# Reordering the convolution stage of a four-layer network: third convolution one step later, three buffers for its input

## The chip, the core and the metric

The kernel runs on one core of a Trainium2 chip. Its engines are TensorE (PE in the profile, matmuls; PEld is its weight load), VectorE (DVE), ScalarE (ACT), GpSimd (POOL) and SyncE (SP). Each has its own instruction stream, and they meet through semaphores. SP and ACT also start transfers. The metric is the device time of one execution in microseconds; lower is better.

## What is computed

Sixty-four images of 16 channels, 128 x 128, pass through four layers. Each normalises its input over pairs of channels and adds its result to the input:

```
x = x + _L0_conv_ref(_gn(x), 5)      # Newton-Schulz inverse, 5 iterations, per channel
x = x + _L1_conv_ref(_gn(x), ...)    # 3x3 convolution of values quantised to whole numbers, scale, bias
x = x + _L2_conv_ref(_gn(x), ...)    # convolution along the diagonal, 5 taps
x = x + _L3_conv_ref(_gn(x), ...)    # 3x3 convolution that wraps around (done there by FFT)
```

The quantisation scale of layer 1 is a maximum over all images. So layer 0 of all images has to end before layer 1 of the first begins.

## The kernel before

The first stage (layer 0 for all images, lines up to 1060) takes about half of the time and is not touched. The second stage holds layers 1 to 3, and here the first, second and third convolution (numbers l = 1, 2, 3).

An image lies in SBUF as 128 partitions (8 rows by 16 channels) by 16 groups of rows by 128 columns. A convolution is worked out in four tiles (`BPI` = 4, index `u`) of 512 columns, each in one PSUM bank: `taps[l]` shifted band matrices on the normalised image `xn{l}`, then one product with the halo rows `xh{l}`, which transfers have gathered from `xn{l}`. Layer 1 needs one bf16 product for each shift, so 3 + 1 = 4 matmuls a tile. Layers 2 and 3 split values and weights into an upper and a lower fp16 part and need three products for each: 15 + 3 = 18 and 9 + 3 = 12 matmuls a tile. Six banks (`B_RING`) go round; `bank_free` makes PE wait for the evacuation of the tile that had the bank before.

What the other engines do for one image and one layer:

- DVE, `residual(l, n, u)` (lines 1251 to 1268): scales bank `u` and adds the layer's input. For l = 1 and 2 `chunk_stats` (1277) takes the statistics of the tile for the next layer, and `whole_stats` (1281) sums them.
- PE, `mean(l, n)` (1405): a small matmul of these sums with `gm`. DVE, `deviations` (1289 to 1299), five short instructions from it. PE, `var` (1410): a small matmul of their result, semaphore `spread`. DVE, `variance` (1303); ACT, `root` (1207); DVE, `normalise` (1312 to 1322), five short instructions and the scaling of the whole image into `F{l}`.
- ACT, `upper` (1202): the fp16 upper part. POOL, `lower` (1164): four instructions for the lower part. For l = 3 ACT copies borders, `wrap` (1192 to 1197), since this convolution wraps around. Then three halo transfers each go out on SP (1130) and on ACT (1184).
- Layer 1 has no statistics of its own here; `quantise` (1243 to 1248, DVE) makes `xn1` in three passes over the image, and ACT adds the bias in place (1214, in `first`) behind its three halo transfers.

The order on each engine is written out by hand, as a `step(s)` that every engine runs for s = 0 to 65 with layers of different images. In step s, PE does convolution 1 of image s, convolution 2 of s-1, convolution 3 of s-2. `mean` and `var` of layer 2 (image s) stand inside convolution 2, and those of layer 3 (image s-1) inside convolution 3. No engine may pass an instruction of its own that waits. The inputs of layers 2 and 3 lie in two buffers each (`x2_0`, `x2_1`, `x3_0`, `x3_1`); the output image takes the place of the third's input and is stored from there (1151), and `out_stored` makes the next writer wait for that store.

```
for u in range(BPI):
    conv(2, s, s - 1, h + odd - 1, 1 - odd, u,
         (lambda: mean(2, s)) if u == 1 and there(s) else None)
    if there(s) and u == 1:
        var(2, s)
```

Of the kernel before, what the change touches and what calls it, by code (L numbers as in the profile page):

```python
# [19 lines left out]
H = 128  # L20
C = 16
G = 8
CPG = C // G
RB = 8
NJ = H // RB
PW = H + 4
L = 2
# [14 lines left out]
def conv_net(nc, x, ident, gmat, gsel, w1, w1h, w2, w2h, w3, w3h, scale_w, bias, x1d, out):  # L42
# [39 lines left out]
    with keep:  # L82
# [982 lines left out]
        with ExitStack() as mem:  # L1065
# [4 lines left out]
            xs = [None, x1s] + [[sb(f"x{l}_{n}", [H, NJ, H]) for n in range(2)] for l in (2, 3)]  # L1070
# [15 lines left out]
            out_stored = [sem(f"out_stored{n}") for n in range(2)]  # L1086
# [16 lines left out]
            FIRST = 4  # L1103

            def run(eng, step):

                for s in range(FIRST):
                    step(s, s // 2, s % 2)
                images(step, FIRST, B - 2, 2)
                for s in range(B - 2, B + 2):  # L1110
                    step(s, s // 2, s % 2)

            def there(i):

                return not isinstance(i, int) or 0 <= i < B

            with nc.Block() as block:

                @block.sync
                def _(sp):  # L1120
                    def halos(l, n, odd):

                        if l == 3:
                            sp.wait_ge(wrapped, 2 * n + 2)
                        else:
                            sp.wait_ge(normed[l], n + 1)
                        for k, (row, shift, _) in enumerate(HALO[l][3:]):
                            r, at = row - RB, 2 * PW + L + shift
                            to = C * (k + 3)
                            sp.dma_start(xh[l][odd][to:to + C, :, 0:RUN],  # L1130
                                         xn[l][odd][C * r:C * r + C, :, at:at + RUN]).then_inc(halo[l][odd], 16)

                    def load(n, h, odd):
                        stand(sp, evac[1], BPI * (n - 1), w_loaded, 16 * 6)
                        sp.dma_start(xs[1][odd][:, :, :],
                                     x1d[n, :, :, 0:H].rearrange("j p w -> p j w")).then_inc(x1_in[odd], 16)

                    halos(1, 0, 0)

                    def step(s, h, odd):  # L1140
                        if there(s - 2):
                            halos(3, s - 2, odd)
                        if there(s + 2):
                            load(s + 2, h + 1, odd)
                        if there(s + 1):
                            halos(1, s + 1, 1 - odd)
                        if there(s):
                            halos(2, s, odd)
                        if there(s - 2):
                            stand(sp, evac[3], BPI * (s - 1), w_loaded, 16 * 6)  # L1150
                            sp.dma_start(out[s - 2, :, :, :], xs[3][odd][:, :, :]).then_inc(out_stored[odd], 16)

                    run(sp, step)
                    for n in range(2):
                        sp.wait_ge(out_stored[n], 16 * (B // 2))

                @block.gpsimd
                def _(pool):

                    def lower(l, n, odd):  # L1160

                        pool.wait_ge(high[l], n + 1)
                        for a in range(0, NJ, 4):
                            ins = nc.gpsimd.tensor_tensor(padded(xn[l][odd], 1)[:, a + 1:a + 5, L:L + H],  # L1164
                                                          F[l][:, a:a + 4, :],
                                                          padded(xn[l][odd], 0)[:, a + 1:a + 5, L:L + H],
                                                          ALU.subtract)
                        ins.then_inc(normed[l], 1)

                    def step(s, h, odd):  # L1170
                        if there(s):
                            lower(2, s, odd)
                        if there(s - 1):
                            lower(3, s - 1, 1 - odd)

                    run(pool, step)

                @block.scalar
                def _(act):
                    def halos(l, n, odd):  # L1180

                        for k, (row, shift, _) in enumerate(HALO[l][:3]):
                            r, at = row + RB, L + shift
                            act.dma_start(xh[l][odd][C * k:C * k + C, :, 0:RUN],  # L1184
                                          xn[l][odd][C * r:C * r + C, :, at:at + RUN]).then_inc(halo[l][odd], 16)

                    def wrap(i, odd):

                        v = xn[3][odd][:, :, :].rearrange("p s (j w) -> p s j w", w=PW)
# [9 lines left out]
                    def upper(l, n, odd):  # L1199

                        act.wait_ge(scaled_f[l], n + 1)
                        nc.scalar.activation(padded(xn[l][odd], 0)[:, 1:NJ + 1, L:L + H], F[l][:, :, :],  # L1202
                                             ACT.Copy).then_inc(high[l], 1)
# [6 lines left out]
                    def first(n, h, odd):  # L1210

                        act.wait_ge(normed[1], n + 1)
                        halos(1, n, odd)
                        nc.scalar.activation(xs[1][odd][:, :, :], xs[1][odd][:, :, :], ACT.Identity,
                                             bias=bst[:, 0:1]).then_inc(biased, 1)

                    def step(s, h, odd):
                        if there(s - 2):
                            wrap(s - 2, odd)
                            act.wait_ge(wrapped, 2 * s - 2)  # L1220
                            halos(3, s - 2, odd)
                        if there(s):
                            root(2, s)
                            upper(2, s, odd)
                        if there(s + 1):
                            first(s + 1, h + odd, 1 - odd)
                        if there(s):
                            act.wait_ge(normed[2], s + 1)
                            halos(2, s, odd)
                        if there(s - 1):  # L1230
                            root(3, s - 1)
                            upper(3, s - 1, 1 - odd)

                    first(0, 0, 0)
                    run(act, step)

                @block.vector
                def _(dve):
                    def quantise(n, h, odd):

                        dve.wait_ge(x1_in[odd], 16 * h + 16)
                        link = Link(dve, q_chain, 2 * n)
                        link.done(nc.vector.tensor_scalar(T[:, :, :], xs[1][odd][:, :, :], mcol[:, bass.ds(n, 1)],
                                                          acol[:, bass.ds(n, 1)], ALU.subtract, ALU.mult))
# [3 lines left out]
                        nc.vector.tensor_scalar(padded(xn[1][odd], 0)[:, 1:NJ + 1, L:L + H], T[:, :, :], MAGIC, -QMAX,  # L1248
                                                ALU.subtract, ALU.max).then_inc(normed[1], 1)

                    def residual(l, n, h, odd, u):

                        a, b = 4 * u, 4 * u + 4
                        bank = banks[(BPI * (l - 1) + u) % B_RING][:, :].rearrange("p (j w) -> p j w", w=H)
                        dst = xs[min(l + 1, 3)][odd][:, a:b, :]
                        dve.wait_ge(conv_ps[l], BPI * n + u + 1)
                        if l == 1:
                            if u == 0:
                                dve.wait_ge(biased, n + 1)
                            nc.vector.scalar_tensor_tensor(out=dst, in0=bank, scalar=sws[:, 0:1],  # L1260
                                                           in1=xs[1][odd][:, a:b, :], op0=ALU.mult,
                                                           op1=ALU.add).then_inc(evac[l], 1)
                        else:
                            if l == 2 and u == 0:
                                need(dve, out_stored[odd], 16 * h)
                            nc.vector.scalar_tensor_tensor(out=dst, in0=bank, scalar=wtop[l]["u"][:, 0:1],  # L1266
                                                           in1=xs[l][odd][:, a:b, :], op0=ALU.mult,
                                                           op1=ALU.add).then_inc(evac[l], 1)
# [5 lines left out]
                    def chunk_stats(l, n, odd, u):  # L1274

                        dve.wait_ge(evac[l - 1], BPI * n + u + 1)
                        nc.vector.bn_stats(bst_[l][:, u, :], xs[l][odd][:, 4 * u:4 * u + 4, :]).then_inc(gchain[l], 1)  # L1277
# [28 lines left out]
                    def normalise(l, n, odd):  # L1306

                        c = cols[l]
                        need(dve, normed[l], n)
# [12 lines left out]
                        nc.vector.tensor_scalar(F[l][:, :, :], xs[l][odd][:, :, :],  # L1322
                                                c["m"][:, 0:1], c["r"][:, 0:1], ALU.subtract,
                                                ALU.mult).then_inc(scaled_f[l], 1)
# [174 lines left out]
```

## Time and profile before

| What | Value |
|---|---|
| Median of three runs | 4287.48 us (4286.44 to 4287.55) |
| Span of the profiled execution, first to last instruction | 4285.7 us |
| Busy share of the span: PE, DVE, POOL, ACT | 98%, 80%, 56%, 48% |
| Second stage, from its first matmul | from 2277.1 us on |
| Mean granted TensorE clock of the core | 0.992 |

For the profiled execution no time of its own is given beside its span; the span is 1.8 us below the median of the runs. Busy time of PE is a poor measure by itself, since matmuls overlap. In the timeline what counts is the distance from one start to the next. A timeline row gives the start, the time from there to the end of the last instruction merged into it, engine, line, operation, result and inputs, shapes, and the number merged; in brackets stands the idle time before it, if it is worth telling, and what ended it.

### The profile page before, as it was taken

How to read it: one execution, taken by the hardware profiler on the slowest of the kernel's cores; microseconds unless marked ns; L12 is line 12 of the kernel's file. 1: busy time of each engine (PE TensorE's matmuls, PEld its weight loads, DVE VectorE, ACT ScalarE, POOL GpSimd, SP SyncE). 2: the span in 40 equal slices, each digit the busy share in tenths (PEclk: the TensorE clock that was granted, in tenths of full speed). 3: DMA queues.
4: the chain of work that ended last, by engine and by line, in shares of the span. 5: the costliest groups of instructions: out<-in, count | busy, mean ns of one | idle time of the engine just before them, and what ended most of it. 6: DMA issues, size and time to landing. Idle time of an engine off the chain costs nothing. (4 is left out here: it accounts for less than half of the span.)

```text
span 4285.7 us, 81705 instructions
## 1 busy us (share of the span) xinstructions
PE 4194.6 (98%) x30409; PEld 3108.7 (73%) x30409; DVE 3444.2 (80%) x7393; ACT 2072.5 (48%) x4296; POOL 2407.9 (56%) x3149
## 2 busy tenths in 40 slices
PE   7999999999999999999996999999999999999998
PEld 7999999999999999999992444444444444444443
DVE  6888888888888888888876787878787888888784
ACT  5776777777777777777761222222222222222221
POOL 6888888888888888888871222222222222222221
PEclk9999999999999999999997999999999999999999
DMA  2221222222222222222214555555555555555553
GB/s 69 64 62 55 65 65 60 60 60 60 60 66 65 60 63 68 60 60 60 60 41 97 133 137 134 137 133 137 134 138 134 138 134 138 134 138 134 138 134 84
DMA packets 333657, 404.28 MB, mean 94 GB/s; under 512 B 23088, under 2 KB 286032, under 8 KB 316880
## 3 DMA queue, kind: packets, MB, share of 16 engines
q1 hardware_dynamic: 308688, 334.25, 30.8%
q10 hardware_dynamic: 24576, 64.79, 5.6%
q8 instruction: 246, 4.03, 0.4%
q14 instruction: 147, 1.20, 0.1%
HBM read 135.22 MB, written 134.22 MB: 63 GB/s over the span
## 5 line engine op out<-in xcount | busy, mean ns | idle before, releaser
L1392 PE MATMUL bank<-xn,wt 128*128 128x512 f16 (+1 forms) x6912 | 1661.6, 381 | 19.9 <-issue 10.7
L1164 POOL TENSOR_TENSOR xn<-F,xn 128x512 f16<-128x512 f32 x512 | 541.6, 1090 | 1453.2 <-ACT xn L1202 1453.2
L1392 PEld LDWEIGHTS bank<-xn,wt 128*128 128x128 f16 (+1 forms) x6912 | 672.9, 100 | 805.0 <-issue 21.9
L463 ACT ACTIVATE P<-bank 128x512 f32<-128x512 f32 x1024 | 606.8, 608 | 264.0 <-PE bank L962 154.5
L1266 DVE SCALAR_TENSOR_TENSOR x<-bank,wu,x 128x512 f32<-128x512 f32 x512 | 382.4, 747 | 313.7 <-PE bank L1399 306.6
L1202 ACT ACTIVATE xn<-F 128x2048 f16<-128x2048 f32 x128 | 244.9, 1913 | 603.3 <-DVE F L1322 603.3
L1399 PE MATMUL bank<-xh,wth 96*128 96x512 f16 (+1 forms) x1792 | 515.6, 380 | 12.1 <-DMA xh<-xn 12.1
L313 POOL TENSOR_TENSOR W<-W 128x512 f16<-128x512 f32 x256 | 290.3, 1166 | 145.7 <-ACT W L489 145.7
L1277 DVE BATCH_NORM_STATS2 bs<-x 128x6 f32<-128x512 f32 x512 | 355.6, 695 | 17.7
L569 DVE BATCH_NORM_STATS2 st<-X 128x6 f32<-128x256 f32 x1024 | 351.5, 411 | 5.8 <-DMA X<-in_x 5.7
L1399 PEld LDWEIGHTS bank<-xh,wth 96*128 96x128 f16 (+1 forms) x1792 | 174.2, 97 | 232.6 <-DMA xh<-xn 15.7
L358 POOL TENSOR_TENSOR S<-P 128x512 f32<-128x512 f32 x256 | 317.8, 1272 | 32.0 <-ACT P L463 31.6
L369 POOL TENSOR_TENSOR P<-P,idt 128x512 f32<-128x512 f32 x256 | 318.4, 1278 | 29.0 <-ACT P L463 28.8
L353 POOL TENSOR_TENSOR YX<-idt,YX 128x512 f32<-128x512 f32 x256 | 324.1, 1278 | 5.5 <-ACT YX L453 5.5
L498 ACT ACTIVATE W<-X,nb,r 128x256 f32<-128x256 f32 x512 | 259.4, 590 | 134.2 <-POOL nb L341 130.7
L1207 ACT ACTIVATE sd<-ve 128x1 f32<-128x1 f32 x128 | 26.1, 204 | 608.9 <-DVE ve L1303 603.0
L364 POOL TENSOR_TENSOR S<-S,P 128x512 f32<-128x512 f32 x256 | 318.1, 1274 | 0.0
L453 ACT ACTIVATE YX<-bank,cs 128x128 f32<-128x128 f32 x1024 | 277.7, 381 | 11.8 <-PE bank L894 3.5
L673 DVE SCALAR_TENSOR_TENSOR X<-bank,cout,X 128x128 f32<-128x128 f32 x1024 | 270.5, 344 | 12.9 <-PE bank L988 12.9
L607 DVE TENSOR_TENSOR P<-bank,idt 128x512 f32<-128x512 f32 x256 | 177.0, 692 | 109.0 <-PE bank L979 103.2
L929 PE MATMUL bank<-YX 128*128 128x128 f32 x2048 | 260.9, 276 | 0.0
L944 PE MATMUL bank<-P 128*128 128x128 f32 x2048 | 260.2, 277 | 0.0
(129 smaller groups left out, 7619.3 us busy)
## 6 DMA issues: line engine op xcount, KB each, us to landing
X<-in_x SPq DMA_DIRECT2D x64, 1024.0 KB, 4.8
x_scratch<-X SPq DMA_DIRECT2D x64, 1024.0 KB, 5.6
X<-x_scratch SPq DMA_DIRECT2D x64, 1024.0 KB, 8.8
out<-x SPq DMA_DIRECT2D x64, 1024.0 KB, 3.9
xh<-xn SPq DMA_DIRECT2D x384, 131.8 KB, 4.5
xh<-xn ACTq DMA_DIRECT2D x384, 131.8 KB, 5.4
xh<-xn SPq DMA_DIRECT2D x192, 65.9 KB, 3.2
xh<-xn ACTq DMA_DIRECT2D x192, 65.9 KB, 2.7
```

The lines of the kernel that those rows point to most:

```text
L313: nc.gpsimd.tensor_tensor(W16[:, 1, at, :], W[:, at, :], W16[:, 0, at, :], ALU.subtract).then_inc(w_lower, 1)
L353: nc.gpsimd.tensor_tensor(e, eyes, e, ALU.subtract).then_inc(a_new, 1)
L358: nc.gpsimd.tensor_tensor(quad(S, q), quad(P1, q), quad(P2, q), ALU.add).then_inc(s_new, 1)
L364: nc.gpsimd.tensor_tensor(quad(S, q), quad(S, q), quad(P3, q), ALU.add).then_inc(q_new, 1)
L369: nc.gpsimd.tensor_tensor(quad(P2, q), quad(P2, q), eyes, ALU.add).then_inc(r_new, 1)
L463: nc.scalar.activation(into[:, 4 * q:4 * q + 4, :], banks[q][:, :].rearrange("p (m w) -> p m w", m=4), ACT.Copy).then_inc(sb, 1)
L569: ins = nc.vector.bn_stats((st0, st1)[k][:, g, :], group_of(X[slot], g))
L1164: ins = nc.gpsimd.tensor_tensor(padded(xn[l][odd], 1)[:, a + 1:a + 5, L:L + H], F[l][:, a:a + 4, :], padded(xn[l][odd], 0)[:, a + 1:a + 5, ...
L1266: nc.vector.scalar_tensor_tensor(out=dst, in0=bank, scalar=wtop[l]["u"][:, 0:1], in1=xs[l][odd][:, a:b, :], op0=ALU.mult, op1=ALU.add).the ...
L1277: nc.vector.bn_stats(bst_[l][:, u, :], xs[l][odd][:, 4 * u:4 * u + 4, :]).then_inc(gchain[l], 1)
L1392: nc.tensor.matmul(bank, wt[l][:, a, k, :], v, start=(k == a == b == 0), stop=False)
L1399: ins = nc.tensor.matmul(bank, wth[l][:, a, :], v, start=False, stop=(a, b) == products[-1])
```

## The change

The steps are laid out anew. PE now does convolution 1 of image s, then convolution 3 of s-3 (it was s-2), then convolution 2 of s-1; there are 67 steps and not 66. The two small matmuls of layer 2 (image s) stand in convolution 3, after its tiles 1 and 3. Those of layer 3 (image s-2) stand ahead of convolution 3 and after its tile 0. DVE's order follows: convolution 1's residuals with `deviations(3, s-2)` among them, then `variance(3)`, `quantise(s+1)`, `normalise(3, s-2)`, then convolution 3's residuals with `deviations(2, s)`, `variance(2)`, `normalise(2, s)` among them, then convolution 2's. ACT adds the bias and sends the halo of image s+1 before `root(2, s)`. Three buffers hold layer 3's input. Bank and predecessor of each tile come from a list of the whole order. Matmuls, element operations, transfers and the engine of each are the same, and so is the first stage.

```diff
-            xs = [None, x1s] + [[sb(f"x{l}_{n}", [H, NJ, H]) for n in range(2)] for l in (2, 3)]
+            THIRD = 3
+            xs = [None, x1s] + [[sb(f"x{l}_{n}", [H, NJ, H]) for n in range(k)] for l, k in ((2, 2), (3, THIRD))]
...
+            LATE = (None, 0, 1, 3)
+            STEPS = B + LATE[3]
...
+            order = [(l, s - LATE[l], u) for s in range(STEPS) for l in (1, 3, 2) if there(s - LATE[l]) for u in range(BPI)]
+            place = {piece: k for k, piece in enumerate(order)}
...
                 def _(sp):
...
+                    for s in range(STEPS):
+                        if there(s - 1):
+                            sp.wait_ge(normed[2], s)
+                            halo_copies(sp, 2, s - 1, False)
+                        if there(s + 2):
+                            load(s + 2)
+                        if there(s + 1):
+                            sp.wait_ge(normed[1], s + 2)
+                            halo_copies(sp, 1, s + 1, False)
+                        if there(s - 3):
+                            store(s - 3)
                         if there(s - 2):
...
+                            sp.wait_ge(wrapped, 2 * (s - 1))
+                            halo_copies(sp, 3, s - 2, False)
...
                 def _(act):
...
+                    first(0)
+                    for s in range(STEPS):
+                        if there(s - 1):
+                            act.wait_ge(normed[2], s)
+                            halo_copies(act, 2, s - 1, True)
                         if there(s - 2):
...
+                            root(3, s - 2)
+                            upper(3, s - 2)
+                        if there(s + 1):
+                            first(s + 1)
                         if there(s):
                             root(2, s)
-                            upper(2, s, odd)
...
+                            upper(2, s)
+                        if there(s - 2):
+                            wrap(s - 2)
+                            act.wait_ge(wrapped, 2 * (s - 1))
+                            halo_copies(act, 3, s - 2, True)
...
                 def _(dve):
...
+                    quantise(0)
+                    for s in range(STEPS):
+                        for u in range(BPI):
+                            if u == BPI - 1 and there(s - 2):
+                                deviations(3, s - 2)
+                            if there(s):
+                                residual(1, s, u)
+                                chunk_stats(2, s, u)
                         if there(s):
...
                             whole_stats(2, s)
+                        if there(s - 2):
+                            variance(3, s - 2)
+                        if there(s + 1):
+                            quantise(s + 1)
+                        if there(s - 2):
+                            normalise(3, s - 2)
                         for u in range(BPI):
...
+                            if there(s - 3):
+                                residual(3, s - 3, u)
                             if there(s):
                                 if u == 0:
                                     deviations(2, s)
-                                if u == 1:
+                                if u == 2:
                                     variance(2, s)
...
+                                if u == 3:
+                                    normalise(2, s)
+                        for u in range(BPI):
+                            if there(s - 1):
+                                residual(2, s - 1, u)
+                                chunk_stats(3, s - 1, u)
                         if there(s - 1):
                             whole_stats(3, s - 1)
...
                 def _(pe):
...
+                    for s in range(STEPS):
                         if there(s):
                             for u in range(BPI):
...
+                                conv(1, s, u)
+                        if there(s - 2):
+                            mean(3, s - 2)
+                        for u in range(BPI):
+                            if there(s - 3):
+                                conv(3, s - 3, u)
+                            if there(s - 2) and u == 0:
+                                var(3, s - 2)
+                            if there(s):
+                                if u == 1:
+                                    mean(2, s)
+                                if u == 3:
+                                    var(2, s)
                         if there(s - 1):
                             for u in range(BPI):
...
+                                conv(2, s - 1, u)
```

The program of the changed kernel shows what this makes of two engines. First PE, in one of the last full steps before the change: convolution 1's last tile, then the beginning of convolution 2 (bank 6 takes the small matmuls of layer 2, bank 7 those of layer 3).

```order
L1399 MATMUL bank3<-xh1_1,wth1 128x512
L1392 MATMUL bank4<-xn2_0,wt2 128x512 x15
L1399 MATMUL bank4<-xh2_0,wth2 128x512 x3
L1392 MATMUL bank5<-xn2_0,wt2 128x512 x6
L1405 MATMUL bank6<-s2,gm 128x1
L1392 MATMUL bank5<-xn2_0,wt2 128x512 x9
L1399 MATMUL bank5<-xh2_0,wth2 128x512 x3
L1410 MATMUL bank6<-q2,gm 128x1
L1392 MATMUL bank0<-xn2_0,wt2 128x512 x15
```

The same engine after the change, from the small matmul behind convolution 1 to the first matmuls of convolution 2 (L1371 and L1376 are the convolution's lines now, L1382 is `mean`, L1387 `var`):

```order
L1382 MATMUL bank7<-s3,gm 128x1
L1371 MATMUL bank0<-xn3_0,wt3 128x512 x9
L1376 MATMUL bank0<-xh3_0,wth3 128x512 x3
L1387 MATMUL bank7<-q3,gm 128x1
L1371 MATMUL bank1<-xn3_0,wt3 128x512 x9
L1376 MATMUL bank1<-xh3_0,wth3 128x512 x3
L1382 MATMUL bank6<-s2,gm 128x1
L1371 MATMUL bank2<-xn3_0,wt3 128x512 x9
L1376 MATMUL bank2<-xh3_0,wth3 128x512 x3
L1371 MATMUL bank3<-xn3_0,wt3 128x512 x9
L1376 MATMUL bank3<-xh3_0,wth3 128x512 x3
L1387 MATMUL bank6<-q2,gm 128x1
```

The small matmul of `q2`, which waits for DVE's `deviations(2)`, has moved from the inside of convolution 2 to the place right ahead of it, and all of convolution 2 stands behind it.

DVE before the change, around `deviations(2)`, which ends with `q2`:

```order
L1277 BN_STATS bs2<-x2_0 128x6
L1281 TENSOR_REDUCE s2<-bs2 128x1
L1266 SCALAR_TENSOR_TENSOR x3_1<-bank4,wu2,x2_1 128x512
L1277 BN_STATS bs3<-x3_1 128x6
L1289 TENSOR_TENSOR dv2<-bs2,bank6 128x8
L1291 COPY m2<-bank6 128x1
L1293 TENSOR_TENSOR dv2<-dv2 128x8
L1295 SCALAR_TENSOR_TENSOR dv2<-bs2,dv2 128x8
L1299 TENSOR_REDUCE q2<-dv2 128x1
```

DVE after it (L1256 is every residual, L1270 `whole_stats`, L1237 to L1242 `quantise`, L1300 to L1311 `normalise`, L1278 to L1288 `deviations`):

```order
L1270 TENSOR_REDUCE s2<-bs2 128x1
L1292 TENSOR_SCALAR ve3<-bank7 128x1
L1237 TENSOR_SCALAR T<-X1,mcol,acol 128x2048
L1240 TENSOR_SCALAR T<-T 128x2048
L1242 TENSOR_SCALAR xn1_1<-T 128x16x128
L1300 RECIPROCAL ra3<-sd3 128x1
L1302 TENSOR_TENSOR rb3<-ra3 128x1
L1304 TENSOR_TENSOR rb3<-rb3,ve3 128x1
L1306 TENSOR_SCALAR rb3<-rb3 128x1
L1308 TENSOR_TENSOR r3<-ra3,rb3 128x1
L1311 TENSOR_SCALAR F3<-x3_0,m3,r3 128x2048
L1256 SCALAR_TENSOR_TENSOR x3_2<-bank0,wu3,x3_2 128x512
```

`deviations(2)` follows behind the last of these rows. Between `s2` and it there stood one residual with its statistics; now there stand `variance(3)`, the three passes of `quantise`, `normalise(3)` and one residual.

## Rows read from the trace of the kernel before

**Rows 1.** Windows: busy us and instructions of each engine, clock, DMA, one step.

```profile
3217.34:3247.87 30.53, 30.48 (x145) 13.99 (x144) 24.59 (x49) 7.48 (x9) 8.46 (x8) 1.00 0.57 136
```

**Rows 2.** Timeline of PE, convolution 2, 3 and 1 of a step.

```profile
3226.30 0.38 PE L1405 MATMUL bank<-s,gm 128*128 128x1 f32 x2
3226.54 2.12 PE L1392 MATMUL bank<-xn,wt 128*128 128x512 f16 x9
...
3233.20 3.43 PE L1392 MATMUL bank<-xn,wt 128*128 128x512 f16 x15
...
3237.12 2.13 PE L1392 MATMUL bank<-xn,wt 128*128 128x512 f16 x9
...
3247.87 0.82 PE L1392 MATMUL bank<-xn,wt 128*128 128x512 bf16 x3
...
3251.39 3.43 PE L1392 MATMUL bank<-xn,wt 128*128 128x512 f16 x15
```

**Rows 3.** Timeline of DVE in the same stretch.

```profile
3220.43 0.75 DVE L1260 SCALAR_TENSOR_TENSOR x<-bank,sws,X 128x512 f32<-128x512 f32 x1
...
3221.82 0.73 DVE L1260 SCALAR_TENSOR_TENSOR x<-bank,sws,X 128x512 f32<-128x512 f32 x1
...
3226.16 0.75 DVE L1266 SCALAR_TENSOR_TENSOR x<-bank,wu,x 128x512 f32<-128x512 f32 x1
...
3227.56 0.14 DVE L1289 TENSOR_TENSOR dv<-bs,bank 128x8 f32<-128x8 f32 x1
...
3228.21 0.16 DVE L1299 TENSOR_REDUCE q<-dv 128x1 f32<-128x8 f32 x1
...
3230.74 0.14 DVE L1303 TENSOR_SCALAR ve<-bank 128x1 f32<-128x1 f32 x1
...
3234.58 0.16 DVE L1312 RECIPROCAL ra<-sd 128x1 f32<-128x1 f32 x1
...
3235.54 1.35 DVE L1322 TENSOR_SCALAR F<-x,m,r 128x2048 f32<-128x2048 f32 x1
3236.81 0.75 DVE L1266 SCALAR_TENSOR_TENSOR x<-bank,wu,x 128x512 f32<-128x512 f32 x1
...
3248.07 0.75 DVE L1266 SCALAR_TENSOR_TENSOR x<-bank,wu,x 128x512 f32<-128x512 f32 x1 [1.94 <-PE bank L1399]
3248.74 0.15 DVE L1312 RECIPROCAL ra<-sd 128x1 f32<-128x1 f32 x1
```

**Rows 4.** Timeline of POOL and DVE, where both are busy.

```profile
3238.91 4.23 POOL L1164 TENSOR_TENSOR xn<-F,xn 128x512 f16<-128x512 f32 x4 [12.14 <-ACT xn L1202]
...
3241.63 0.49 DVE L1293 TENSOR_TENSOR dv<-dv 128x8 f32<-128x8 f32 x1
3242.16 1.01 DVE L1295 SCALAR_TENSOR_TENSOR dv<-bs,dv 128x8 f32<-128x8 f32 x1
```

**Rows 5.** Timeline, start of the stage, to PE's first step with all three convolutions.

```profile
2281.36 0.61 PE L1399 MATMUL bank<-xh,wth 96*128 96x512 bf16 x1 [2.80 <-DMA xh<-xn]
...
2288.17 0.16 DVE L1281 TENSOR_REDUCE s<-bs 128x1 f32<-128x8 f32 x1
...
2300.38 0.61 PE L1399 MATMUL bank<-xh,wth 96*128 96x512 bf16 x1 [4.40 <-DMA xh<-xn]
...
2305.69 3.43 PE L1392 MATMUL bank<-xn,wt 128*128 128x512 f16 x15
...
2362.64 0.82 PE L1392 MATMUL bank<-xn,wt 128*128 128x512 bf16 x3
```

**Rows 6.** Timeline, end of the program, from the last of the full steps on.

```profile
4224.67 3.43 PE L1392 MATMUL bank<-xn,wt 128*128 128x512 f16 x15
...
4253.05 1.34 DVE L1322 TENSOR_SCALAR F<-x,m,r 128x2048 f32<-128x2048 f32 x1
...
4268.99 1.46 PE L1399 MATMUL bank<-xh,wth 96*128 96x512 f16 x3 [3.54 <-DMA xh<-xn]
4270.24 4.05 PE L1392 MATMUL bank<-xn,wt 128*128 128x512 f16 x9
```

More of the change, by code:

```diff
@@ L1102, in conv_net, with xs_of, bank_of, halo_copies @@
             CH = 9
[L1103 to L1111, printed above, removed]
-            def there(i):
-                return not isinstance(i, int) or 0 <= i < B
+            LATE = (None, 0, 1, 3)
+            STEPS = B + LATE[3]
+            def there(i):
+                return 0 <= i < B
+            def xs_of(l, n):
+                return xs[l][n % len(xs[l])]
+            order = [(l, s - LATE[l], u) for s in range(STEPS) for l in (1, 3, 2) if there(s - LATE[l]) for u in range(BPI)]
+            place = {piece: k for k, piece in enumerate(order)}
+            def bank_of(l, n, u):
+                return banks[place[l, n, u] % B_RING]
+            def halo_copies(eng, l, n, above):
+                for k, (row, shift, _) in enumerate(HALO[l]):
+                    if (row < 0) == above:
+                        r, at = row % RB, (0 if row < 0 else 2 * PW) + L + shift
+                        eng.dma_start(xh[l][n % 2][C * k:C * k + C, :, 0:RUN],
+                                      xn[l][n % 2][C * r:C * r + C, :, at:at + RUN]).then_inc(halo[l][n % 2], 16)
             with nc.Block() as block:
@@ L1120, in _ @@
                 def _(sp):
[L1121 to L1131, printed above, removed]
@@ L1153, in _, with load, store @@
-                    run(sp, step)
-                    for n in range(2):
-                        sp.wait_ge(out_stored[n], 16 * (B // 2))
+                    def load(n):
+                        stand(sp, evac[1], BPI * (n - 1), w_loaded, 16 * 6)
+                        sp.dma_start(xs_of(1, n)[:, :, :],
+                                     x1d[n, :, :, 0:H].rearrange("j p w -> p j w")).then_inc(x1_in[n % 2], 16)
+                    def store(n):
+                        sp.wait_ge(evac[3], BPI * (n + 1))
+                        sp.dma_start(out[n, :, :, :], xs_of(3, n)[:, :, :]).then_inc(out_stored[n % THIRD], 16)
@@ L1171, in step @@
                         if there(s):
[L1172 to L1176, printed above, removed]
+                            lower(2, s)
                 @block.scalar
                 def _(act):
[L1180 to L1185, printed above, removed]
@@ L1256, in residual @@
                         dve.wait_ge(conv_ps[l], BPI * n + u + 1)
[L1257 to L1268, printed above, removed]
+                        if l == 1 and u == 0:
+                            dve.wait_ge(biased, n + 1)
@@ L1348, in step @@
+                        for u in range(BPI):
+                            if there(s - 1):
+                                residual(2, s - 1, u)
+                                chunk_stats(3, s - 1, u)
                         if there(s - 1):
                             whole_stats(3, s - 1)
-                        for u in range(BPI):
-                            if there(s - 2):
-                                residual(3, s - 2, hb, before, u)
-                            if there(s - 1):
-                                if u == 0:
-                                    deviations(3, s - 1)
-                                if u == 2:
-                                    variance(3, s - 1)
-                                if u == 3:
-                                    normalise(3, s - 1, prev)
@@ L1377, in conv, with bank_free @@
-                    def conv(l, s, n, h, odd, u, between=None):
-                        bank = banks[(BPI * (l - 1) + u) % B_RING][:, :]
+                    def bank_free(l, n, u):
+                        k = place[l, n, u] - B_RING
+                        if k >= 0:
+                            m, i, v = order[k]
+                            pe.wait_ge(evac[m], BPI * i + v + 1)
+                    def conv(l, n, u):
+                        bank = bank_of(l, n, u)[:, :]
                         if u == 0:
```

149 lines of the change are left out of this document (42 added, 107 removed).

## The prediction, as it was made before the run

> **What bounds the kernel now.** I read the windows first. One step of the second stage lasts 30.53 us, PE is busy for 30.48 us of it at full clock, and DVE for 24.59 us [rows 1]. So PE bounds the steady part, and a new order of the same work can win next to nothing there. The timeline of PE then tells what a step holds. A tile of convolution 2 takes 3.92 us (3233.20 to 3237.12). Convolution 3 with two small matmuls in it takes 10.75 us (3237.12 to 3247.87), and convolution 1 takes 3.52 us (3247.87 to 3251.39) [rows 2]. Four tiles of convolution 2 are 15.67 us. 15.67 + 10.75 + 3.52 = 29.94 us; the other 0.59 us are the two small matmuls in convolution 2, the first of which waits a little for DVE and costs 0.24 us once it starts (3226.30 to 3226.54) [rows 2]. Full steps follow each other from 2362.64 us [rows 5] to 4224.67 us [rows 6]: 1862.0 us for 61 steps, 30.53 each. Any wait of PE that the new order puts into a step counts 61 times; the rest is the start and the drain.
>
> **The steady step, laid out by hand.** The place to look at is the small matmul of `q2`. It now stands ahead of all of convolution 2, and DVE has much to do before it delivers `q2`. Let 0 be the moment at which PE ends the last tile of convolution 2 and begins convolution 1. DVE has been idle there (it needs about 1.4 us a tile against 3.92) and starts 0.20 us later: 3248.07 against 3247.87 [rows 2, 3]. From there DVE never waits, so its instructions follow at the distances in rows 3:
> - last tile of convolution 2 and `whole_stats(3)`: a residual with statistics takes 1.38 us (3220.43 to 3221.82), and four of these with the sum 5.73 us (3220.43 to 3226.16), so the sum adds 0.20. DVE is at 0.20 + 1.38 + 0.20 = 1.78.
> - three tiles of convolution 1: 3 x 1.38 = 4.15, to 5.93. PE has ended these tiles by 2.6 us, so none is waited for.
> - `deviations(3)`: 0.65 to its last instruction (3227.56 to 3228.21), 0.16 for that, and the next starts 0.08 behind its start: to 6.66; `q3` is there at 6.74.
> - fourth tile and `whole_stats(2)`: 1.58, to 8.24.
> - `variance(3)` and `quantise`: 3.84 (3230.74 to 3234.58), to 12.08.
> - `normalise(3)`: 2.23 (3234.58 to 3236.81), to 14.31. Its root on ACT has 3.8 us beside `quantise`.
> - one residual without statistics: 0.67 (3248.07 to 3248.74), to 14.98.
> - `deviations(2)`: 0.65 + 0.16, so `q2` is there at 15.79.
>
> PE has 3.52 us of convolution 1, the small matmul of `s3` (about 0.15), and 10.75 us of convolution 3. On its way it meets `q3`: tile 0 of convolution 3 ends at about 3.67 + 2.62 = 6.29, and `q3` comes at 6.74, so it loses 0.5 and the slower start of a matmul that waited, 0.1. It stands at the matmul of `q2` at about 15.0. `q2` comes 0.8 us later. With 0.06 for the semaphore and the 0.24 of a waiting small matmul, convolution 2 starts at 16.1, and the step ends at 16.1 + 15.67 = 31.8 us. I take 31.78. The first wait (for `q3`) is swallowed by the second, since DVE and not PE sets the time of `q2`. What bounds a step is then a ring: last tile of convolution 2, DVE's row of work, `q2`, convolution 2. The step is 1.25 us longer, 61 x 1.25 = 76 us.
>
> **What is moved and costs nothing.** Layer 3 gets a whole step between `normalise(3)` and its convolution. From the start of `F` to the landed halo this chain took 15.94 us at the end of the program (4253.05 to 4268.99) [rows 6]; in the new step it starts at 13.0 and would end at 29, but its border copies stand behind `upper(2)` on ACT, which puts them some 4 us later: 33. PE asks for this halo at 31.8 + 5.6 = 37.4, in tile 0 of the next step. This is the thinnest cover, 4 us; a halo later than that adds what it is late. ACT's queue is the other: the bias of image s+1 and its three transfers now stand ahead of `root(2)`. DVE's `normalise(2)` waits there from about 17.8 to about 20, and behind it are the residuals of convolution 2. It has to end before 31.98 less three tiles, 27.8, so 5 us of slack cover it; past that each us costs one. The image for `quantise` is loaded a step ahead, the store has a step more through the third buffer, and all banks come free 1.5 us or more before PE asks. On SP each transfer stands behind a wait that is over by then. These I cost at nothing.
>
> **Start and drain.** Before, the first full step starts at 2362.64 [rows 5]. In the new order DVE ends the sum for image 0 at 2288.17 as before, quantises image 1 at once (to 2292), and then comes ACT's work (three transfers and the bias, about 4.2 us) ahead of the root; `normalise(2, 0)` ends at about 2298.8. PE can finish convolution 1 of image 1 at about 2292.0 + 4.3 (wait of 2.80 for the halo and three cold matmuls [rows 5]) + 5.3 (2300.38 to 2305.69) = 2301.6. Four tiles on DVE, `quantise` and `deviations` end at 2298.8 + 5.7 + 3.8 + 0.8 = 2309.1; `q2` blocks convolution 2 here too. It starts at 2309.5 and not at 2305.69, and ends at 2325.2 or, with a clock fallen to half after such idle time, 2.4 us later. Step 2 has no convolution 3, and lasts 31.1 us with PE idle for most of the first 15; again up to 2.4 us for the clock. (Cold matmuls take 1.25 us for three, 4268.99 to 4270.24 [rows 6], against 0.65 warm; some 12 of them are 2.4 us.) So the first full step starts between 2356 and 2361; I take 2361, since PE idles in both places. The 61 full steps end at 2361 + 61 x 31.78 = 4299.6. Step 64 has no convolution 1: about 2.2 us until `s3`, 10.6, 15.67, together 28.5. Then `F` of the last image starts 6.5 us after its convolution 2 (tile and sum 1.8, small matmul, `deviations`, root and five short instructions), its halo lands 15.9 later, and from there on it is as before: 4285.7 - 4269.0 = 16.7. Together 39.1. The end is 4299.6 + 28.5 + 39.1 = 4367.2, against the profiled span of 4285.7: 81.5 more. The median of the runs is 1.8 above that span, so 4287.5 + 81.5 = 4369; with the last tiles a little warmer than before I say **4368 us**.
>
> **Rivals.** (1) *DVE and POOL meet.* In the old order `deviations` meets POOL's `lower` once a step, and two of its instructions take 0.49 and 1.01 us [rows 4] where both take about 0.2 without POOL [rows 3]; the second ends within 0.1 us of POOL's end (3238.91 + 4.23). If this happened to `deviations(2)` in the new order, it would add some 1.15 us to the ring: 4368 + 61 x 1.15 = 4438. It speaks against it that POOL starts 3.37 us after the start of `F` (3235.54 to 3238.91 [rows 3, 4]), so at 13.04 + 3.37 = 16.4 in my step, 0.6 us after `q2`. The rival decides if DVE is over 0.6 us later between `F` and `q2` than I have it. The Trainium skill (SBUF — State Buffer, Who interferes with whom) says that a DVE instruction with two SBUF inputs and a GpSimd one that reads SBUF share a read path which one holds for its whole instruction; the trace agrees, with 1.01 us for an instruction that takes 0.17 alone.
>
> (2) *Not slower.* *PE stays the bound.* If DVE delivered `q2` 0.8 us earlier than I have it, and `q3` 0.5 us earlier, PE would stay the bound: 29.94 us, which hold two of the small matmuls, and two more at about 0.14 make 30.22 us a step, less than the 30.53 now, because the wait in front of the matmul at 3226.30 [rows 2] goes too. Then 2361 + 61 x 30.22 + 28.5 + 39.1 = 4272, or **4274** as a median, 0.3% faster than before. The point from which this decides is a DVE row of 15.0 us from the end of convolution 2 to `q2`. For it: it needs only 5% less. Against it: every distance in the row was measured in the same chain of instructions without idle time.
>
> (3) *The clock falls* in the new pauses of under 1 us. If only one tile of convolution 2, 18 matmuls, ran at half clock, each step would lose 3.7 us: 4594. A wait of this kind is in the old order with 0.2 us only and the clock stayed at 1.00 [rows 1].
>
> **How the numbers follow.** The forecast has 83%, the meeting with POOL 6%, the PE-bound step 9%, the clock 2%. The forecast's own bounds are 0.4 us a step either way (24 us: some distances are read from other pairs of instructions) and 6 us for the start and drain: about 4340 to 4400. This holds its 83% nearly whole; the others lie outside, and the range ends there. About 0.2% (8.6 us) is what a measurement of this kernel can tell from no change. Slower: the forecast, POOL and the clock, 91%. The PE-bound step is faster by over 0.2% where both waits vanish (5%), and within 0.2% where 0.1 to 0.3 us of them stay in each step (4%).
>
> **What would show it.** Right: a window of one step of 31.8 us with PE idle before L1387 for 0.4 to 0.5 us and again for 0.8, released by DVE's L1288; DVE without idle time from the last residual of convolution 2 to L1288, idle before `normalise(2)` for about 2 us, released by ACT. POOL's first instruction starts after L1288 has ended. Wrong: a PE that waits on halo transfers, on `normed`, or on banks; L1284 at 1 us; a clock below 1.00 in the steady part; or a step of 30.2 to 30.5 us.

## The result, and the profile after

The changed kernel takes 4371.28 us (4371.05 to 4372.48, 4 runs) against 4286.96 us before (4286.03 to 4287.55, 4 runs). The ratio is 1.0198, with a 95% interval of 1.0184 to 1.0213: slower by 84 us. The profiled execution spans 4369.8 us.

The windows view of one full step after the change answers to [rows 1] (columns as there: window, length, busy us and instructions of PE, PEld, DVE, ACT and POOL, clock, DMA share, GB/s).

```profile
3218.88:3250.64 31.76, 30.73 (x145) 13.91 (x144) 25.00 (x49) 7.24 (x9) 8.47 (x8) 1.00 0.56 131
```

The same 145 matmuls at the same clock of 1.00 now take 31.76 us and not 30.53. The waits view of the changed kernel, from 2400 to 4250 us, names what PE waits for (in total, times, longest):

```profile
DVE x L1256 <- PE bank L1376: 300.6, 175, 2.4
PEld bank L1387 <- DVE q L1288: 117.1, 116, 1.2
PE bank L1387 <- DVE q L1288: 60.2, 117, 0.7
DVE ra L1300 <- ACT sd L1203: 36.7, 58, 0.7
```

PEld's row is the weight load of the same matmul, which overlaps PE. There are two waits a step (117 in 58 steps), both of the small matmul of `q` (L1387) for the last of DVE's `deviations` (L1288). The timeline of PE shows where they are (in brackets: idle time before, and what ended it). It answers to [rows 2]:

```profile
3218.88 0.82 PE L1371 MATMUL bank<-xn,wt 128*128 128x512 bf16 x3
...
3224.50 0.81 PE L1376 MATMUL bank<-xh,wth 96*128 96x512 f16 x3
3225.69 0.38 PE L1387 MATMUL bank<-q,gm 128*128 128x1 f32 x2 [0.38 <-DVE q L1288]
3225.93 2.13 PE L1371 MATMUL bank<-xn,wt 128*128 128x512 f16 x9
...
3233.28 0.81 PE L1376 MATMUL bank<-xh,wth 96*128 96x512 f16 x3
3234.74 0.38 PE L1387 MATMUL bank<-q,gm 128*128 128x1 f32 x2 [0.65 <-DVE q L1288]
3234.98 3.43 PE L1371 MATMUL bank<-xn,wt 128*128 128x512 f16 x15
...
3250.64 0.82 PE L1371 MATMUL bank<-xn,wt 128*128 128x512 bf16 x3
```

Three halo matmuls take 0.65 us from start to next start, so convolution 3 ends at 3233.93 and the small matmul starts 0.81 us later (the bracket says 0.65, since the modelled end of a matmul lies after its successor's start). DVE's timeline in the same step answers to [rows 3], and POOL's first row stands with it:

```profile
3219.08 0.75 DVE L1256 SCALAR_TENSOR_TENSOR x<-bank,wu,x 128x512 f32<-128x512 f32 x1 [2.44 <-PE bank L1376]
...
3225.47 0.16 DVE L1288 TENSOR_REDUCE q<-dv 128x1 f32<-128x8 f32 x1
...
3230.98 0.16 DVE L1300 RECIPROCAL ra<-sd 128x1 f32<-128x1 f32 x1
...
3231.94 1.35 DVE L1311 TENSOR_SCALAR F<-x,m,r 128x2048 f32<-128x2048 f32 x1
...
3234.32 0.17 DVE L1284 SCALAR_TENSOR_TENSOR dv<-bs,dv 128x8 f32<-128x8 f32 x1
3234.52 0.16 DVE L1288 TENSOR_REDUCE q<-dv 128x1 f32<-128x8 f32 x1
...
3237.35 0.16 DVE L1300 RECIPROCAL ra<-sd 128x1 f32<-128x1 f32 x1 [0.63 <-ACT sd L1203]
3237.55 0.96 DVE L1302 TENSOR_TENSOR rb<-ra 128x1 f32<-128x1 f32 x1
3238.55 1.01 DVE L1304 TENSOR_TENSOR rb<-rb,ve 128x1 f32<-128x1 f32 x1
```

```profile
3235.31 4.23 POOL L1169 TENSOR_TENSOR xn<-F,xn 128x512 f16<-128x512 f32 x4 [19.51 <-ACT xn L1198]
```

From 3219.08, where convolution 2 has released it, DVE has no idle time until it delivers `q2`. It first waits behind that, before `normalise(2)` (0.63 us, for the root on ACT). `deviations` runs at its short durations, since POOL begins 0.63 us after L1288 has ended. It is `normalise(2)` that meets POOL: L1302 and L1304 take 0.96 and 1.01 us where 0.16 is usual (L1300, ahead of them, still takes it). PE does not wait for that: its next tiles follow each other without a gap, and DVE is idle again before the second residual of convolution 2, from 3242.71 to 3243.01.

### The profile page after: what moved, and what is told of

It is laid out like the page before. It is cut to its first block and busy times, and to the rows that moved or that the text cites. A ratio compares the mean times of both kernels' runs of the same rounds, so it can differ in the third digit from the quotient of the medians.

```text
span 4369.8 us, 81640 instructions
## 1 busy us (share of the span) xinstructions
PE 4217.2 (97%) x30409; PEld 3105.2 (71%) x30409; DVE 3470.4 (79%) x7393; ACT 2055.8 (47%) x4296; POOL 2407.3 (55%) x3149
## 5 line engine op out<-in xcount | busy, mean ns | idle before, releaser
L1371 PE MATMUL bank<-xn,wt 128*128 128x512 f16 (+1 forms) x6912 | 1649.4, 383 | 7.7 <-DVE xn L1242 5.2
L1371 PEld LDWEIGHTS bank<-xn,wt 128*128 128x128 f16 (+1 forms) x6912 | 674.5, 100 | 797.9 <-issue 21.6
L1256 DVE SCALAR_TENSOR_TENSOR x<-bank,wu,x 128x512 f32<-128x512 f32 x512 | 375.6, 746 | 368.5 <-PE bank L1376 368.3
L1376 PE MATMUL bank<-xh,wth 96*128 96x512 f16 (+1 forms) x1792 | 515.8, 380 | 8.3 <-DMA xh<-xn 8.3
L1376 PEld LDWEIGHTS bank<-xh,wth 96*128 96x128 f16 (+1 forms) x1792 | 174.5, 97 | 228.8 <-DMA xh<-xn 10.6
```

Source lines behind the costliest of these rows:

```text
L1256: nc.vector.scalar_tensor_tensor(out=dst, in0=bank, scalar=col[:, 0:1], in1=xs_of(l, n)[:, at, :], op0=ALU.mult, op1=ALU.add).then_inc(eva ...
L1371: nc.tensor.matmul(bank, wt[l][:, a, k, :], v, start=(k == a == b == 0), stop=False)
L1376: ins = nc.tensor.matmul(bank, wth[l][:, a, :], v, start=False, stop=(a, b) == products[-1])
```

## Experiments

Two theories stood against each other. Mine: DVE's row of work between the end of convolution 2 and `q2` closes a ring with convolution 2, and the place of the small matmuls decides. The rival: the order as such (the steps, the third buffer, the transfers) costs the time, and the wait is only where it shows. All kernels but one start from the changed kernel.

**q2's small matmul behind tile 0 of convolution 2.**

```diff
-                                if u == 3:
-                                    var(2, s)
-                        if there(s - 1):
-                            for u in range(BPI):
+                        for u in range(BPI):
+                            if there(s - 1):
                                 conv(2, s - 1, u)
+                            if there(s) and u == 0:
+                                var(2, s)
```

> The changed order, with the small matmul of q2 moved on PE from ahead of convolution 2 to behind its tile 0. My theory (the ring through DVE's row and q2 sets the step): the wait of 0.8 us and the slower small matmul behind it go, the wait for q3 (0.54 + 0.10 us) stays, so the step falls from 31.76 to about 30.85 us; with some 10 us less at the start, where q2 no longer blocks convolution 2, about 4306 us. Rival (the longer step comes from the order as such, the third buffer or the transfers, and the wait is only where it shows): the wait reappears elsewhere and the time stays near 4371.

Measured: 4306.62 us (4305.68 to 4310.10, 3 runs). The order, the buffers and the transfers are those of the changed kernel, so the rival falls. The step is 30.85 us (from 2354.63 to 2385.48, the starts of convolution 1), as expected, with the one wait for `q3` in it. That the median comes out at the expected 4306 is in part chance: in the profiled execution, the longest of the three (4310.10), the start is 6.6 us shorter than in the changed kernel and not 10.

**The opposite way round: DVE's `deviations(2)` ahead of `normalise(3)`, PE untouched.**

```diff
                             quantise(s + 1)
+                        if there(s):
+                            deviations(2, s)
                         if there(s - 2):
                             normalise(3, s - 2)
...
-                                if u == 0:
-                                    deviations(2, s)
```

> The changed order, with DVE's deviations(2) moved ahead of normalise(3) and the residual; PE as in the changed kernel. My theory: q2 is there at about 12.9 us of the step, before PE asks at 15.0, so only the wait for q3 stays; 30.85 us a step, about 4314 us. Rival (order as such): near 4371.

Measured: 4314.40 us (4313.24 to 4315.55, 2 runs), step 30.84 us (2358.10 to 2388.94). The wait can be taken away from either end. The profiled execution spans 4311.6 us and that of the run before 4308.4. These 3.2 us lie ahead of the first full step (2358.10 against 2354.63). The medians are 8 us apart, but the three executions of the run before differ by 4.4 us among themselves, and no trace shows where the rest beyond the 3.2 us lies.

**Only q3's small matmul moved.**

```diff
-                            if there(s - 2) and u == 0:
+                            if there(s - 2) and u == 1:
                                 var(3, s - 2)
```

> The changed order, with only the small matmul of q3 moved, behind tile 1 of convolution 3; q2 stays ahead of convolution 2. My theory (DVE's row sets q2): PE waits less for q3, but DVE's variance(3) gets its value 0.96 us later, at 9.2 us of the step, and all behind it down to q2 moves by that; step 32.7 us, about 4429 us, slower although a wait is gone. Rival (each wait of PE costs its own length): 0.64 us less a step, about 4332 us.

Measured: 4513.56 us (4513.31 to 4513.82, 2 runs). A wait of PE is gone, and the kernel is 142 us slower. This settles that waits don't simply add up here, but the size was off by 85 us. The timeline of PE in this kernel shows both parts:

```profile
3216.76 0.82 PE L1371 MATMUL bank<-xn,wt 128*128 128x512 bf16 x3
...
3230.61 0.81 PE L1376 MATMUL bank<-xh,wth 96*128 96x512 f16 x3
3233.58 0.38 PE L1387 MATMUL bank<-q,gm 128*128 128x1 f32 x2 [2.17 <-DVE q L1288]
3233.83 5.09 PE L1371 MATMUL bank<-xn,wt 128*128 128x512 f16 x15
3238.76 0.81 PE L1376 MATMUL bank<-xh,wth 96*128 96x512 f16 x3
3239.41 3.43 PE L1371 MATMUL bank<-xn,wt 128*128 128x512 f16 x15
...
3251.15 0.82 PE L1371 MATMUL bank<-xn,wt 128*128 128x512 bf16 x3
```

`q2`'s matmul starts at 3233.58 - 3216.76 = 16.82 us of the step, where the ring puts it (15.86 + 0.96). But after 2.3 us without matmuls tile 0 of convolution 2 takes 5.58 us (3233.83 to 3239.41) and the next one its usual 3.92. The first matmuls run at 1.2 GHz and not at 2.4: the windows view has a granted clock of 0.65 for the 15 matmuls of this tile (3233.83 to 3238.76), and of 0.95 over 400 us of the kernel:

```profile
3200.00:3600.00 400.00, 376.17 (x1689) 169.05 (x1688) 291.88 (x569) 84.41 (x106) 101.31 (x96) 0.95 0.51 121
```

Sixty of the 61 full steps hold this pause (in the last there is no `quantise` of a next image ahead of `deviations(2)`, and `q2` is there in time). In 8 of the 60 the matmuls behind it are not slow, and the step lasts 32.73 us, just what was expected. The other 52 last 34.36 us in the mean: 52 x 1.63 = 85 us, which is the missing amount. Why the same pause costs in one step and not in another is not shown.

**Both small matmuls of q moved** (the first and the third edit together).

> As the run before, and the small matmul of q3 behind tile 1 of convolution 3 instead of tile 0. My theory: no wait of PE is left in a step, 30.2 us, about 4267 us, less than the kernel before the change (4287). Rival (order as such): not below 4350.

Measured: 4278.61 us (4275.20 to 4279.96, 9 runs), ratio to the kernel before the change 0.9977 (0.9966 to 0.9987). So the new order beats the old one once no small matmul stands before its input. It beats it by less than I said. The full steps run from 2357.06 to 4207.48 us, 30.33 us each and not 30.2: `q3`'s and `s2`'s small matmuls now stand in a row, and take 0.37 us from the start of the first to the next tile, where two apart take 0.14 each:

```profile
3214.53 0.28 PE L1387 MATMUL bank<-q,gm 128*128 128x1 f32 x2
3214.68 0.36 PE L1382 MATMUL bank<-s,gm 128*128 128x1 f32 x2
3214.90 2.13 PE L1371 MATMUL bank<-xn,wt 128*128 128x512 f16 x9
```

The 0.09 us more are 5.5 us in 61 steps. Some 2 us come from four single steps that are 0.3 to 0.9 us longer; in three of them PE waits 0.3 to 0.8 us for the halo in tile 0 of convolution 3 (at 3302.91, 3727.95 and 4152.50). The start (from the stage's first matmul to the first full step, 2278.53 to 2357.06) is 6.5 us shorter than in the changed kernel (2276.17 to 2361.18), where I had expected 10 for the move of `q2`'s matmul.

**Meeting POOL.** Rival 1 of the prediction asked what happens if `deviations(2)` comes later on DVE. Two kernels put it behind one and behind two more residuals:

```diff
-                                if u == 0:
+                                if u == 1:
                                     deviations(2, s)
```

> The changed order, with DVE's deviations(2) behind one more residual of convolution 3. My theory of the ring without POOL: q2 comes 0.66 us later, and so does the step, 32.4 us, about 4411 us. DVE's L1284 would end at 16.3 us of the step and POOL's lower begins at 16.4. If the two engines meet already here: over 33 us a step, about 4470 us.

Measured: 4408.45 us (4407.93 to 4408.97, 2 runs), step 32.43 us (2392.72 to 2425.15). The ring follows DVE by exactly the one residual, and PE's pause of 1.5 us leaves the clock at 1.00. POOL starts at 3219.84, 0.16 us after the end of L1284, so the two just miss each other.

```diff
-                                if u == 0:
+                                if u == 2:
                                     deviations(2, s)
-                                if u == 2:
+                                if u == 3:
                                     variance(2, s)
-                                if u == 3:
                                     normalise(2, s)
```

> The changed order, with DVE's deviations(2) behind two more residuals, so that its two-input instructions fall into POOL's lower. If an instruction of DVE with two inputs in SBUF waits there for the running one of POOL's four: q2 at about 18.8 us of the step, 34.7 us a step, about 4551 us. If the two do not disturb each other: 1.33 us more than the changed kernel, 33.1 us, about 4452 us.

Measured: 4718.30 us (4717.63 to 4718.97, 2 runs). The timelines of DVE and POOL in this kernel (POOL's row holds three of its four instructions, to the end of the stretch shown):

```profile
3243.88 3.18 POOL L1169 TENSOR_TENSOR xn<-F,xn 128x512 f16<-128x512 f32 x3 [25.10 <-ACT xn L1198]
3244.00 0.98 DVE L1282 TENSOR_TENSOR dv<-dv 128x8 f32<-128x8 f32 x1
3245.02 1.01 DVE L1284 SCALAR_TENSOR_TENSOR dv<-bs,dv 128x8 f32<-128x8 f32 x1
3246.07 0.16 DVE L1288 TENSOR_REDUCE q<-dv 128x1 f32<-128x8 f32 x1
```

DVE's L1282 starts 0.12 us after POOL's first instruction and ends 1.10 us after that start, when POOL's first (1.06 us) is over, and L1284 ends with POOL's second; the reduction, which reads one tensor, is not held. The Trainium skill (SBUF — State Buffer, Who interferes with whom) calls the read and write ports that DVE shares with GpSimd an exclusive lock, and says that a DVE instruction with two SBUF inputs contends with a GpSimd one that reads SBUF. The trace agrees: 0.98 and 1.01 us for two instructions that take 0.17 each without POOL. `q2`'s matmul starts at 18.84 us of the step (3246.28 - 3227.44), where 18.8 was expected. The 167 us that the kernel is slower than expected are the clock again, as PE's timeline shows:

```profile
3246.28 0.58 PE L1386 MATMUL bank<-q,gm 128*128 128x1 f32 x2 [3.62 <-DVE q L1288]
3246.73 6.02 PE L1370 MATMUL bank<-xn,wt 128*128 128x512 f16 x15
3252.59 0.81 PE L1375 MATMUL bank<-xh,wth 96*128 96x512 f16 x3
3253.24 3.43 PE L1370 MATMUL bank<-xn,wt 128*128 128x512 f16 x15
```

Tile 0 takes 6.51 us and not 3.92. The 2.6 us more are 158 us in 61 steps, and 4551 + 158 = 4709. The small matmul itself is slow too (0.45 us to the next start and not 0.24), which adds 13 us at most; with it the sum is 4722, 4 us over the measured time.

**What the old order leaves.** The wait of 0.2 us before the matmul at 3226.30 [rows 2] is in the kernel before. One edit there moves the small matmul of `s2` three matmuls on:

```diff
-                            if between and k == 1:
+                            if between and k == (2 if l == 2 else 1):
                                 between()
```

> The kernel before the change, with one edit: the small matmul of s2 stands after nine matmuls of tile 1 of convolution 2 instead of six. Theory: the old step holds one wait of 0.22 us and 0.10 us of slower start, which go: 30.2 us a step, 61 x 0.32 = 19.5 us, about 4267.5 us. Rival (the wait only moves to q2 or to DVE's chain): 4287.

Measured: 4266.04 us (4265.89 to 4271.84, 4 runs), ratio 0.9953 (0.9938 to 0.9967). The full step is 30.21 us (2366.30 to 4209.15, 61 steps), 0.32 less than before.

**All small matmuls of the new order off their waits.** `s3` and `q3` behind tiles 0 and 1 of convolution 3, `q2` as in the first experiment:

```diff
-                        if there(s - 2):
-                            mean(3, s - 2)
                         for u in range(BPI):
                             if there(s - 3):
                                 conv(3, s - 3, u)
-                            if there(s - 2) and u == 0:
-                                var(3, s - 2)
+                            if there(s - 2):
+                                if u == 0:
+                                    mean(3, s - 2)
+                                if u == 1:
+                                    var(3, s - 2)
```

> The changed order, with q2's small matmul behind tile 0 of convolution 2, and those of s3 and q3 behind tiles 0 and 1 of convolution 3. Theory: step 30.2 us as with q2 and q3 moved alone, and at the end PE no longer stands before s3 in the steps without convolution 1, where it idled twice for 1.8 us and then ran some 3.5 us at half clock: 7 us less than that run, about 4260 us. Rival (the idle time at the end is only moved, since the last image's chain sets the end): about 4267 us.

Measured: 4271.46 us (4269.74 to 4272.64, 5 runs), 7.1 us less than with the two of `q` alone. I had expected 4260, which was 7 us less than the 4267 expected of that run, and that run had missed its 4267. Part of the gain is where it was expected: from the end of the full steps to the end of the span it is 65.6 us (4203.75 to 4269.3) and not 70.6 (4207.48 to 4278.1). These are 5.0 of the 8.8 us between the two profiled spans. The other 3.7 lie ahead of the end of the full steps (2.9 of them ahead of the first, 2354.18 against 2357.06) and were not expected. So the near match of 7.1 with the 7 expected is in part chance.

Last, `s2`'s matmul behind tile 2, so that no two stand in a row:

```diff
-                                if u == 1:
+                                if u == 2:
                                     mean(2, s)
```

> As the run with all three small matmuls moved, and that of s2 behind tile 2 of convolution 3 instead of tile 1, where it stood right behind q3's. Theory: two small matmuls in a row cost 0.36 us against 0.28 apart, and with them apart the full step falls from 30.32 us to 30.21, 61 x 0.11 = 6.7 us; about 4265 us, level with the old order with its one edit (4266) or a little less. Rival (the step is held by DVE's row by now): 4271.

Measured: 4266.17 us (4264.13 to 4268.11, 4 runs), ratio 0.9952 (0.9935 to 0.9968); step 30.22 us (2355.16 to 4198.75, 61 steps). The best new order and the old one with its one edit can't be told apart: with these places of the small matmuls, the order of the convolutions is worth nothing that can be measured.

## Why the prediction was right

The forecast was 4368 us, and 4371.28 was measured. Point by point:

- **The ring.** `q2` was put at 15.79 us of the step, and L1288 ends at 3234.52 + 0.16 - 3218.88 = 15.80. `q3` was put at 6.74, and comes at 6.75. Convolution 2 was to start at 16.1, and does at 3234.98, which is 16.10. The step was to be 31.78 and is 31.76. The full steps carry 75 us of the 84. The other 9 are the two ends: the first full step begins 1.5 us earlier than before (2361.18 against 2362.64), and from the end of the full steps to the end of the span it is 71.4 us and not 61.0.
- **The first wait is swallowed by the second.** Right, by the kernel with only `q3`'s matmul moved: with this wait gone, `q2` came no sooner but 0.96 us later.
- **The POOL rival.** POOL was put at 16.4 us, and starts at 16.43. As forecast, it did not happen. But the rival's own numbers were off. It was to decide at 0.6 us, counted to the end of `q2`; the run with one more residual was 0.67 us later and missed POOL. Both runs fit if it is the last instruction with two inputs in SBUF that counts, L1284, which ends at 3234.49, 0.82 us ahead of POOL. The price was put at 1.15 us a step, and the meeting costs 1.65 in the run with two more residuals (0.98 and 1.01 us against 0.17 each), because both instructions fall wholly into POOL's. Its total of 4438 was too low for that reason, and more so because the clock falls too.
- **ACT's queue.** `normalise(2)` was to wait about 2 us for the root, and waited 0.63; ACT's three transfers and bias take less than I had added up, since the three are issued (3233.33 to 3235.18) while ACT works on `upper(3)` (3233.32 to 3235.23). That the two engines would meet there was not foreseen. There was slack for all of it.
- **Third layer's halo.** No wait of PE for a halo is in the full steps, as said. That this is the thinnest cover shows in the shorter steps of the experiments, where PE waited for it a few times.
- **The PE-bound rival.** Its condition did not come about, but its step of 30.22 us was right: it is the step of the last experiment, in which no small matmul waits.
- **The clock rival.** The steady clock stayed at 1.00 with pauses of 0.5 and 0.8 us. The price of 3.7 us for a slow tile was too high: 1.66 and 2.6 us in the two experiments in which the clock fell, since only a part of the tile is slow. In the drain, on the other hand, I left such a cost out.
- **The start.** The first full step was put at 2361 and begins at 2361.18. Part of this is chance: the stage itself began 0.9 us earlier than before. Measured from its first matmul it took 85.0 us against my 83.9.
- **The drain is the mis-sized term.** Step 64 was put at 28.5 us and the rest at 39.1; they take 30.1 (4298.36 to 4328.48) and 41.3. PE's timeline of step 64 shows why:

```profile
4300.29 0.38 PE L1382 MATMUL bank<-s,gm 128*128 128x1 f32 x2 [1.77 <-DVE s L1270]
4300.54 3.70 PE L1371 MATMUL bank<-xn,wt 128*128 128x512 f16 x9
4304.03 0.95 PE L1376 MATMUL bank<-xh,wth 96*128 96x512 f16 x3
```

After 1.9 us without matmuls the nine of tile 0 take 3.49 us and not 1.97, at a granted clock of 0.55. I had counted the pause and not the slow matmuls behind it. The same comes again in step 65, where it also puts off `q3`'s small matmul, which stands behind tile 0, and with it the last image's whole chain: its halo lands 24.6 us after its convolution 2 (4353.10 - 4328.48) and not 22.4. Together 3.8 us were missed; the full steps, 31.757 us each (2361.18 to 4298.36) and not 31.78, give 1.4 back (0.9 of it because the last of them has no `quantise` on DVE, so `q2` comes in time and the step lasts 30.85), and in all the span is 2.6 us over mine.

What the term is worth in one execution is in part chance. The same pause at the same place left the matmuls at full speed in 4 of the 14 cases that the seven profiled executions with `s3`'s small matmul ahead of convolution 3 hold. One of them is step 64 of the kernel with both small matmuls of `q` moved:

```profile
4209.41 0.38 PE L1382 MATMUL bank<-s,gm 128*128 128x1 f32 x2 [1.77 <-DVE s L1270]
4209.65 2.13 PE L1371 MATMUL bank<-xn,wt 128*128 128x512 f16 x9
4211.62 0.81 PE L1376 MATMUL bank<-xh,wth 96*128 96x512 f16 x3
```

No run shows what decides this.

## What to carry to other kernels

When a busy engine must wait for a small result, ask what is queued behind the waiting instruction, and write down the producer's queue from the moment that this same engine releases it: here the sum of start-to-start distances gave the new step to 0.02 us. PE was busy nearly all of a step, so a new order of the same work had only the small waits to win; these (0.3 us a step) went in the old order by moving one small matmul three places, and in the new order by moving four. And a pause of TensorE can cost twice: once itself, and once in slow matmuls behind it, though not every time.

## What the runs showed of the chip

Pauses of PE of 0.8 us (changed kernel) and 1.5 us (`deviations(2)` one residual later) in each step left the granted clock at 1.00. A pause of 2.3 us brought tile 0 from 3.92 to about 5.6 us in 52 of 60 steps and cost nothing in the other 8. One of 3.8 us brought it to 6.51, and no step escaped. One of 1.9 us at the end brought nine matmuls from 1.97 to between 2.6 and 3.6 us in 10 of 14 cases. What lies between 1.5 and 1.9 us was not tried. I had not expected that pauses this short, which recur among 30 us of dense matmuls, bring the clock down at all.
